# A selective-scan kernel: the first scan asks only for the first order's rows and table

## What is computed

```
x_dbl = einsum('bkdl,kcd->bkcl', xs, x_proj_w)          # per position: 12 values for delta, 16 of B, 16 of C
delta = softplus(dts @ dt_w + dt_b)
h[t]  = h[t-1] * exp(delta[t] * A) + (delta[t] * u[t]) * B[t]
y[t]  = sum over n of h[t] * C[t]                       # then + u * D
```

## Time and profile before

| | |
|---|---|
| median of three runs | 15295.29 us (15293.58 to 15296.45) |
| profiled execution, its own time | 15298.41 us |
| its span, first to last instruction | 15296.6 us |
| busy: TensorE, VectorE, ScalarE, GpSimd | 86%, 84%, 72%, 69% of the span |
| granted TensorE clock, mean | 0.968 |
| one image, GpSimd's delta times u of the first chunk to the same of the next image | 1894.45 us (2048.70 to 3943.15) |

### The profile page before, as it was taken

The page is one execution under the profiler, slowest core; times in us unless marked ns, Lnnn a source line. Parts: engine busy times, 40 slices in busy tenths (PEclk is TensorE's granted clock), DMA queues, the critical chain, the costliest instruction groups (busy, mean ns, idle before and its releaser), DMA issues.

```text
span 15296.6 us, 237874 instructions
## 1 busy us (share of the span) xinstructions
PE 13084.6 (86%) x60888; PEld 7840.4 (51%) x60888; DVE 12871.7 (84%) x13813; ACT 11081.7 (72%) x22746; POOL 10502.7 (69%) x4158
## 2 busy tenths in 40 slices
PE   6888888889888888888988889888898888988889
PEld 4555455554555545555455554555445554455544
DVE  8999669996799857998589984899849998499984
ACT  5887578875788657886578866788667886678865
POOL 6998069980699707997079960899608995099950
PEclk9999999999999999999999999999999999999999
DMA  3433023430334303342034420334203342044420
GB/s 111 129 129 114 20 93 129 138 96 20 97 129 138 92 20 103 129 138 87 20 111 129 136 80 20 115 129 136 75 20 120 129 135 71 20 129 129 132 65 25
DMA packets 907942, 1467.94 MB, mean 96 GB/s; under 512 B 38912, under 2 KB 891904, under 8 KB 893664
## 3 DMA queue, kind: packets, MB, share of 16 engines
q1 hardware_dynamic: 906560, 1452.37, 29.9%
HBM read 1350.07 MB, written 102.17 MB: 95 GB/s over the span
## 4 chain that ended last, share of the span: by engine, by line
PE 31%; issue 22%; POOL 19%; DVE 18%; ACT 5%; DMA 4%; DVEq 1%; ACTq 0%; POOLq 0%; SPq 0%
POOL area L1490 14%; DVE area L1013 13%; PE ps L838 9%; PE ps L849 8%; POOL area L1500 5%; PE ps L654 4%; DMA area<-bc_rows 4%; DVE area L1031 3%; ACT ps L1294 1%; PE ps L584 1%; PE ps L752 1%; PE ps L729 1%; PE ps L641 1%; ACT ps L1255 1%; PE ps L712 1%
## 5 line engine op out<-in xcount | busy, mean ns | idle before, releaser
L1013 DVE TENSOR_TENSOR_SCAN area<-ps,hst,area 128x384 f32<-128x384 f32 x9216 | 8571.3, 993 | 116.4 <-POOL area L1490 48.8
L1490 POOL TENSOR_TENSOR area<-area 128x1152 f32<-128x1152 f32 x3072 | 8001.9, 2638 | 50.3 <-POOL area L1479 38.1
L1294 ACT ACTIVATE ps<-area,a_neg 128x384 f32<-128x384 f32 x9216 | 5289.3, 580 | 1148.0 <-DVE area L1013 1087.8
L654 PE MATMUL ps<-area,ident 128*128 128x384 f32 x12672 | 4610.8, 501 | 790.4 <-POOL area L1500 722.0
L654 PEld LDWEIGHTS ps<-area,ident 128*128 128x128 f32 x12672 | 2277.6, 193 | 2506.5 <-POOL area L1500 947.2
L1474 POOL TENSOR_TENSOR area<-area,ones 128x2304 f32<-128x2304 f32 x8 | 43.3, 5417 | 3521.5 <-ACT area L1219 3399.9
L641 PE MATMUL ps<-ident,area 128*128 128x128 f32 x17280 | 2420.8, 277 | 5.2 <-ACT area L1263 5.2
L1433 ACT ACTIVATE area<-ps,t_neg,area 128x768 f32<-128x768 f32 x1728 | 1617.7, 986 | 984.6 <-PE ps L838 984.6
L641 PEld LDWEIGHTS ps<-ident,area 128*128 128x128 f32 x17280 | 2195.1, 193 | 58.9 <-ACT area L1263 9.5
L1500 POOL TENSOR_TENSOR area<-area 128x1152 f32<-128x1152 f32 x768 | 2024.8, 2636 | 34.7 <-ACT hst L1239 34.7
L1263 ACT ACTIVATE area<-ps,area 128x384 f32<-128x384 f32 x2880 | 1637.4, 569 | 535.1 <-PE ps L632 531.5
(11 more groups left out here) (128 smaller groups left out, 9606.7 us busy)
## 6 DMA issues: line engine op xcount, KB each, us to landing
area<-bc_rows SPq DMA_DIRECT2D x1536, 768.0 KB, 6.8
xz<-x_normed SPq DMA_DIRECT2D x144, 288.0 KB, 6.3
area<-in_x SPq DMA_DIRECT2D x18, 1728.0 KB, 10.4
area<-x_padded SPq DMA_DIRECT2D x24, 1250.0 KB, 5.6
z_raw<-z_st SPq DMA_DIRECT2D x144, 192.0 KB, 6.2
area<-z_raw SPq DMA_DIRECT2D x8, 3456.0 KB, 15.0
x_padded<-x_st SPq DMA_DIRECT2D x120, 200.0 KB, 7.7
x_normed<-area SPq DMA_DIRECT2D x9, 1728.0 KB, 7.9
```

The source lines that it names most:

```text
L654: m = e.matmul(ps[:, 5 + j, 0:CH], ident[:], hb[:, i % NH, j], start=i == 0, stop=i == N - 1)
L1013: e.tensor_tensor_scan(rev(hb[:, i % NH, j], k), rev(ps[:, 2 + j, 0:CH], k), rev(dbu[:, i % NH, j], k), hst[:, i, j:j + 1], ALU.mult, ALU. ...
L1294: e.activation(ps[:, 2 + j, 0:CH], dlt[:, par, j], ACT.Exp, scale=a_neg[:, j, k, i:i + 1]).then_inc(da, 1)
L1490: e.tensor_tensor(dbu[:, i % NH], du[:, par], row_b[:, q % 2, i % ROWS:i % ROWS + 1].broadcast_to([128, J, CH]), ALU.mult).then_inc(dbus, 1)
```

## The change

The diff does the following:

- Blocks 2 to 5 of the second order go to banks 6 and 7 instead of 2 and 3 (`xp_bank`). Ahead of block 2, TensorE waits for VectorE's three delta tiles of the first chunk, which were made through those banks.
- The first scan no longer waits for all twelve blocks and the whole table. ScalarE waits for eight blocks (`xp_dv` and `xp_ev` at 10) and the first order's table (`ct_cp` at 3). TensorE waits for the first order's table before the scan, and for the second ahead of step m = 3 of the first chunk.
- ScalarE's row copies 2 to 5 of the second order leave the front and stand in the first chunk behind exponentials (0,2), (1,0), (1,2) and (2,0). Behind exponential (2,2) it waits for the whole table.
- VectorE's row copies 3, 4 and 5 stand behind scans (0,0), (0,2) and (1,0) of the first chunk, and the three groups of the second table behind the scans of state 2. Row copy 2 stays in the front.
- SyncE's and GpSimd's streams are not changed.

```diff
+LATE_ROWS = {(0, 2): 2, (1, 0): 3, (1, 2): 4, (2, 0): 5}
+LATE_STAGE = {(0, 0): 3, (0, 2): 4, (1, 0): 5}
...
+        def xp_bank(o, c):
+            return 6 + c % 2 if o == 1 and c >= 2 else 2 * o + c % 2
...
# TensorE, x_proj
+                    if o == 1 and c == 2:
+                        alone(e)
+                        e.wait_ge(dp_v, b * 72 + 3)
                     for j in range(J):
-                        m = e.matmul(ps[:, 2 * o + c % 2, 0:CH], w_xp[:, j, o], u_v[:, o, j, c * CH:(c + 1) * CH],
+                        m = e.matmul(ps[:, xp_bank(o, c), 0:CH], w_xp[:, j, o], u_v[:, o, j, c * CH:(c + 1) * CH],
...
# TensorE, scan_phase
-                e.wait_ge(ct_cp, b * GM + GM)
+                e.wait_ge(ct_cp, b * GM + 3)
...
+                        if m == 3 and not last:
+                            alone(e)
+                            e.wait_ge(ct_cp, b * GM + GM)
                         slot(g, m)
...
# VectorE, front
-                c_columns(0)
-                for c in range(2, NC):
-                    stage_rows(1, c)
-                c_columns(1)
+                for q in range(3):
+                    c_columns(b, q)
+                stage_rows(b, 1, 2)
...
# VectorE, scan_phase, behind the scan of tile (i, j)
+                            if not last and (i, j) in LATE_STAGE:
+                                stage_rows(b, 1, LATE_STAGE[i, j])
+                            if not last and i == 2:
+                                c_columns(b, 3 + j)
...
# ScalarE, front
-                for c in range(NC):
-                    dt_rows(1, c)
+                dt_rows(b, 1, 0)
+                dt_rows(b, 1, 1)
...
# ScalarE, scan_phase
-                e.wait_ge(xp_dv, b * 12 + 14)
-                e.wait_ge(ct_cp, b * GM + GM)
+                e.wait_ge(xp_dv, b * 12 + 10)
+                e.wait_ge(xp_ev, b * 12 + 10)
+                alone(e)
+                e.wait_ge(ct_cp, b * GM + 3)
...
# behind the exponential of tile (i, j)
+                            if not last and (i, j) in LATE_ROWS:
+                                dt_rows(b, 1, LATE_ROWS[i, j])
+                            if not last and (i, j) == (2, 2):
+                                e.wait_ge(ct_cp, b * GM + GM)

```

More of the change, by code:

```diff
@@ L959, in delta, with stage_rows, c_columns @@
                                        op0=ALU.max, op1=ALU.add).then_inc(dp_v, 1)
+            def stage_rows(b, o, c):
+                e.wait_ge(xp_mm, b * 12 + (6 * o + c + 1))
+                e.tensor_copy(stage[:, o, c * CH:(c + 1) * CH], ps[0:4 * N, xp_bank(o, c), 0:CH]).then_inc(xp_dv, 1)
+            def c_columns(b, q):
+                o, t0, n, bank = ct_group(q)
+                e.wait_ge(ct_mm, b * GM + (q + 1))
+                for a in range(2):
+                    m = e.tensor_copy(c_t[:, o * MT + t0:o * MT + t0 + n, N * a:N * a + N],
+                                      ps[:, bank, 0:64 * n].rearrange("p (t r) -> p t r", r=4 * N)
+                                      [:, :, 2 * N * a + N:2 * N * a + 2 * N])
+                m.then_inc(ct_cp, 1)
             def front(b):
@@ L964, in by_columns @@
                     e.tensor_copy(o, u).then_inc(uwh, 1)
[L966 to L979, removed]
                 e.wait_ge(xn_out, b * 16 + 16)
@@ L983, in front @@
                 by_columns(0)
-                stage_rows(0, 0)
+                stage_rows(b, 0, 0)
                 by_columns(2)
                 for c in range(1, NC):
-                    stage_rows(0, c)
+                    stage_rows(b, 0, c)
                 for j in range(J):
                     delta(e.snap(b * 24), 0, j, 5 + j)
-                stage_rows(1, 0)
-                stage_rows(1, 1)
+                stage_rows(b, 1, 0)
+                stage_rows(b, 1, 1)
                 wait_stored(e, b)
                 alone(e)
-                c_columns(0)
-                for c in range(2, NC):
-                    stage_rows(1, c)
-                c_columns(1)
+                for q in range(3):
+                    c_columns(b, q)
+                stage_rows(b, 1, 2)
             def scan_phase(b):
@@ L1207, in softplus, with dt_rows @@
                     e.activation(ps[:, bank, 0:CH], y, ACT.Ln, bias=1.0).then_inc(dp_a, 1)
+            def dt_rows(b, o, c):
+                e.wait_ge(xp_mm, b * 12 + (6 * o + c + 1))
+                e.activation(dts[64 - 64 * o:128 - 64 * o, c * CH:(c + 1) * CH], ps[64:128, xp_bank(o, c), 0:CH],
+                             ACT.Copy).then_inc(xp_ev, 1)
             def front(b):
[L1210 to L1213, removed]
                 alone(e)
@@ L1223, in front @@
                 e.wait_ge(xn_out, b * 16 + 16)
-                dt_rows(0, 0)
-                dt_rows(0, 1)
+                dt_rows(b, 0, 0)
+                dt_rows(b, 0, 1)
                 for j in range(J):
@@ L1229, in front @@
                     if n % 2 == 0 and n < 8:
-                        dt_rows(0, 2 + n // 2)
+                        dt_rows(b, 0, 2 + n // 2)
                     softplus(g0, 0, 0, op, j, 5 + j)
-                for c in range(NC):
-                    dt_rows(1, c)
+                dt_rows(b, 1, 0)
+                dt_rows(b, 1, 1)
             def scan_phase(b):
```

## The result

| | before | after |
|---|---|---|
| median of ten runs | 15294.74 us (15292.33 to 15296.45) | 15256.07 us (nine of them 15247.98 to 15260.84) |
| profiled execution, its own time | 15298.41 us | 15255.69 us |
| its span | 15296.6 us | 15253.8 us |
| granted TensorE clock, mean | 0.968 | 0.971 |

The ratio is 0.9974, 95% interval 0.9964 to 0.9984: 38.7 us less, where 34.7 were forecast. One of the ten executions of the changed kernel, of 16968.84 us, is left out of the ratio.

The account below looks back on a forecast made before the run. GpSimd and VectorE, both nearly full, bound the scan, GpSimd setting the pace by a little. Closing its 4.33 us gap in eight images takes 34.7 us off 15295.3, nothing added: 15260.6 us, range 15254 to 15283.

Parts of the forecast that it names:

- 1, first scan: First chunk's start: after three exponentials, row copy 2 and GpSimd's first product with B, first scan at 54.2, 8.3 us earlier.
- 3, row copy 5: VectorE's copies 3 to 5 between scans, copy 5 at 59.1 to 59.6; SyncE's store follows at 59.7, costing nothing.
- 4, ScalarE reads delta's tile: Next chunk's delta tile, made after the second table's turn, is read at 62.65; new stall puts scan (2,1) at 63.75, not 62.8.
- 5, scan (3,0): Six table copies between state 2's scans hold ScalarE: second stall of 0.8 us, scan (3,0) at 67.1, scan (4,0) at 71.15.
- The gap closes whole, 34.7 us: GpSimd's 4.33 us wait before state 0's product with C goes in all eight images: 15260.6 us, chance 0.62.
- The margin at state 3, 0.4 to 0.7 us: State 3's copy done at 71.5 to 71.8, GpSimd comes at 72.17; margin was 2.0 us before, shrinks but holds.
- TensorE's first sum: Waits for the second table at 66.35; at its slow 3.34 us done at 69.8, ahead of scan (4,0).
- The new stalls on ScalarE and VectorE cost nothing: First chunk's waits for delta's tile and the table copies (0.8 us) leave GpSimd's gain whole, nothing added to the time.
- VectorE's copies beside GpSimd, price zero: Moved copies amid GpSimd's work taken as free; if each held GpSimd for its length, the gain is 12 us, 15283.
- VectorE sets the pace: From the first chunk on only VectorE's 3.5 us count: 28 us off, 15267; chance 0.22, shared with part of the gap.
- doesn't do what it says: Exponentials or scans held by something overlooked; GpSimd's gap moves from state 0 to state 3: 15290 to 15296, chance 0.10.
- clock in the late blocks: TensorE's 24 late matmuls at 1.2 GHz take 15.4 us, 7.4 more, delaying state 3: 15316; slower, chance 0.06 in all.

Follow-up runs that it names:

- experiment 5: Kernel before plus fifteen matmuls per image in the attention, output read by nobody, to hold the clock up: 15251.16 us, ratio 0.9971.
- experiment 6: Changed kernel plus the same attention fillers as experiment 5: 15219.44 us, ratio 0.995 against the kernel before.
- experiment 2: Changed kernel with all row copies back ahead of the first exponential, only the second table late: 15298.01 us, ratio 1.0 against the kernel before.
- experiment 7: Changed kernel with delta's tile made behind block 3 and ScalarE's whole-table wait moved behind exponential (4,0): 15250.57 us, ratio 0.997.
- experiment 8: On top of experiment 7, softplus first on ScalarE, deltas between VectorE's row copies, late copies one place on: 15234.79 us, ratio 0.9961.
- experiment 9: On top of experiment 8, TensorE does state 1's second turn before waiting for the second table and summing state 0: 15236.04 us, ratio 0.9963.
- experiment 4: Changed kernel plus one 1.34 us VectorE product per image, in the first chunk ahead of state 5's product: 15247.71 us, ratio 0.9969.
- experiment 3: Kernel before plus one 2.6 us GpSimd product per image, in the first chunk, into scratch: 15290.33 us, ratio 0.9997.

## Why the prediction was right

The likeliest case held: 15260.6 forecast, 15256.07 measured, in the range, on the side that was given 0.57. By its steps (times after 2000 us, with 4.98 added to after's):

| step | forecast | measured |
|---|---|---|
| 1, first scan | 54.2 | 54.42 |
| 3, row copy 5 | 59.1 | 59.01 |
| 3, store of the rows issued | 59.7 | 59.63 |
| state 0's copy on ScalarE, its end | 58.8 | 58.83 |
| 4, ScalarE reads delta's tile | 62.65, a stall ended by TensorE | 62.44, after 2.33 idle |
| 4, scan (2,1) | 63.75 | 63.53 |
| 5, scan (3,0) | 67.1 | 66.84, after 0.82 idle |
| 5, scan (4,0) | 71.15 | 70.84 |
| state 3's copy on ScalarE, its start | done at 71.5 to 71.8 | starts 72.20 |
| first sum on TensorE | 3.34 us long | 4.20 us long |
| idle before the products with C | nearly 0 | 2.2 us |

- **The gap closes whole, 34.7 us:** right, but for 2.2 us. By scans it is 33.5, by experiments 5 and 6 it is 31.7.
- **The margin at state 3, 0.4 to 0.7 us:** mis-sized. The copy, 0.20 us long, ended at 72.40, 0.6 to 0.9 us later than stepped, and GpSimd waits about 0.3 us. What the steps left out is the second turn of state 1: it stands on TensorE behind the late sum, and ScalarE waits 1.00 us for it (2066.23) ahead of the copy of state 3. The prediction took the sum as a danger for scan (4,0) alone. Experiment 2 shows how near this was: without the lead of the moved row copies the whole gain goes there.
- **TensorE's first sum:** 0.9 us longer than taken from the earlier trace rows. The 3.34 us there are not the lower level, as the prediction reads them, but a mix: the granted clock over that sum is 0.65. Here it runs wholly at the lower level (granted clock 0.50 between 2061.0 and 2065.5) after 3.53 us without work, twice the 2.10 us of the higher. It still ended at 2065.47, ahead of scan (4,0) at 2065.86. The cover held by 0.4 us; in experiments 7, 8 and 9 it didn't (0.57 us of wait in the first, 2.39 in the other two).
- **The new stalls on ScalarE and VectorE cost nothing:** nearly right. Without them the 2.2 us before the products with C are gone and the eight scans are 1.7 us shorter in all (experiment 7).
- **VectorE's copies beside GpSimd, price zero:** right. Four products with B took 10.37 us (10.35 before) with copies out of PSUM beside them, and all products kept their mean.
- **SyncE's store, price zero:** right; 59.63 against 59.64.
- **Rival "VectorE sets the pace":** refuted by experiment 4. **Rival "doesn't do what it says":** not here, but real, as experiment 2 shows. **Rival "clock in the late blocks":** no; the 24 matmuls took 8.01 us again. Its price was too small: the 0.64 us for a matmul at the lower level is in no row, and the late sum has 4.20 / 6 = 0.70, or 16.8 us for 24 instead of 15.4.
- **Missing in the forecast:** that stages which no line of the diff touches change with the granted clock. It gave 5 to 7 us here; by experiment 5 it can give 44 us, more than the change itself. I took the 3.1 us between the profiled execution and the median for all the spread there was. That these 5 to 7 us went the way of the change is luck; without them the time would have been 15261 to 15263, still in the range. The reason given for the range's lower end did not come true: the gaps at chunk starts did not shrink, GpSimd's idle time before the products with B is 50.3 us in both kernels.

What stays open: why a given image has a short or a long attention stage. The starts of the stages differ between kernels and images, and the lengths with them, but no run set the start alone.

## What to carry to other kernels

A wait that stands once per image is worth nearly its length (33.5 us of 34.7 here) on the engine that never waits again until the end; step the hand-overs behind it by hand up to the next point where that engine asks for something, because there the gap comes back if the lead is spent (experiment 2). When one engine's wait is moved, look at everything that stands behind it in that engine's order: here the second table's wait also held a turn that another engine needed (experiments 8 and 9). When the change is some tenths of a per cent, compare stage by stage, since a stage that wasn't edited can move by as much through TensorE's clock. A few matmuls ahead of a burst that follows light work can be worth more than a reordering (44 us here against 31.7 to 33.5).

## What the hardware showed that was not expected

- The same attention stage took between 480.6 and 486.6 us (GpSimd's idle time) in one execution, by how early the granted clock rose from 1.2 to 2.4 GHz at two bursts: eight matmuls of 64x384 in 2.93 or in 1.56 us, 36 of 128x2 in 7.68 or in 4.57. With fifteen filler matmuls per image it was 478 to 481 us in every image, and the whole kernel 44 us shorter.
- So 17 us of added work on the engine that sets the pace (experiment 3) left the total unchanged, and 13 us less (experiment 9) too.
- A sum of six matmuls of 128x384 took 2.10 us at a granted clock of 1.00 and 4.20 us at 0.50 (after 1.67 to 3.53 us without a matmul, in experiment 9 and the changed kernel). The 3.34 us of the earlier trace rows are a sum within which the clock rose, 0.65 in the mean.
